# First attention of a two-layer attention and mixture-of-experts kernel: VectorE's share of a batch element's four steps dealt anew, the second normalisation moved to it, head outputs turned first

## The reference

```
x = x + xcond0(LN(x), ctx, tau, delta)       # softmax((q.k * tau + delta) / 4) over 375 keys, 16 heads
x = x + moe0(LN(x))                           # 64 experts, 8 chosen per token, sigmoid scores, plus a shared expert
x = x + xcond1(LN(x), ctx, tau, delta)
x = x + moe1(LN(x))                           # 8 experts, 2 chosen per token
```

## Time and profile before

| | |
|---|---|
| median of 3 runs | 1327.96 us (1319.44 to 1330.2) |
| the profiled execution | 1326.04 us, of which the span is 1324.4 us |
| TensorE busy | 1220.1 us, 92% |
| VectorE, GpSimd, ScalarE busy | 823.4, 557.1, 494.9 us |
| mean granted TensorE clock | 0.96 |
| GpSimd, mean of one normalisation (L1857), of one scatter (L1882) | 1254 ns, 968 ns |
| stages, from the span's start | attention 0 to about 377, experts to 676, attention to 1046, experts to 1324 |

### The profile page before, as it was taken

The page is one execution under the profiler, slowest core; times in us unless marked ns, Lnnn a source line. Parts: engine busy times, 40 slices in busy tenths (PEclk is TensorE's granted clock), DMA queues, the critical chain, the costliest instruction groups (busy, mean ns, idle before and its releaser), DMA issues. The chain is left out here.

```text
span 1324.4 us, 40274 instructions
## 1 busy us (share of the span) xinstructions
PE 1220.1 (92%) x12798; PEld 943.0 (71%) x12799; DVE 823.4 (62%) x2642; ACT 494.9 (37%) x1255; POOL 557.1 (42%) x706
## 2 busy tenths in 40 slices
PE   3899999999977999999888999999998999999995
PEld 2566666666644888898645666666666889999995
DVE  2357777877766666666564687777765544444442
ACT  1355454554430344443223544454544122122221
POOL 1116566665565000100356677776732313333231
PEclk8799999999978999999977999999998999999998
DMA  5343444446445668875423343333313313344323
GB/s 139 108 127 121 145 133 136 128 146 192 133 129 165 191 184 233 257 221 158 118 78 84 87 109 92 100 101 94 99 51 144 109 37 101 99 142 124 106 33 82
DMA packets 114268, 166.65 MB, mean 126 GB/s; under 512 B 26288, under 2 KB 95120, under 8 KB 113024
## 3 DMA queue, kind: packets, MB, share of 16 engines
q0 software_dynamic: 22672, 58.41, 17.0%
q1 hardware_dynamic: 46496, 54.35, 14.0%
q10 hardware_dynamic: 45024, 52.98, 12.6%
HBM read 87.82 MB, written 63.49 MB: 114 GB/s over the span
## 5 line engine op out<-in xcount | busy, mean ns | idle before, releaser
L1039 DVE TENSOR_REDUCE mx<-banks 112x2 f32<-112x750 f32 x256 | 235.3, 934 | 109.9 <-PE banks L625 96.8
L1882 POOL DMA_INDIRECT xs_d<-xns,idx x160 | 154.9, 968 | 136.6 <-PE banks L647 90.6
L1557 ACT ACTIVATE shared_buf<-banks 125x672 f32<-125x672 f32 x256 | 173.1, 728 | 104.3 <-PE banks L647 103.7
L1896 POOL DMA_INDIRECT kept<-y_d,yidx x128 | 124.7, 974 | 104.6 <-issue 83.3
L911 PEld LDWEIGHTS banks<-xT,attn_buf 128*128 128x128 f32 x1364 | 157.1, 192 | 4.8 <-DVE xT L1423 3.2
L911 PE MATMUL banks<-xT,attn_buf 128*128 128x128 f32 x1364 | 157.4, 275 | 3.0 <-DVE xT L1423 3.0
L856 PE MATMUL banks<-xT,staged 128*128 128x128 f32 x1064 | 142.7, 277 | 6.7 <-DVE staged L1434 6.2
L647 PE MATMUL banks<-attn_buf 18*125 18x112 f32 x3072 | 122.4, 290 | 24.7 <-DVE mx L1039 20.0
L856 PEld LDWEIGHTS banks<-xT,staged 128*128 128x128 f32 x1064 | 129.1, 192 | 11.6 <-DVE xT L1423 7.6
L647 PEld LDWEIGHTS banks<-attn_buf 18*125 18x125 f32 x3072 | 99.6, 189 | 53.0 <-DVE mx L1039 28.2
L625 PE MATMUL banks<-attn_buf 17*112 17x375 f32 x1024 | 119.7, 538 | 12.9 <-DMA attn_buf<-qT 10.1
(11 more groups left out here) (214 smaller groups left out, 1901.4 us busy)
## 6 DMA issues: line engine op xcount, KB each, us to landing
shared_buf<-xs_d SPq DMA_DIRECT2D x136, 128.0 KB, 2.4
y_d<-shared_buf ACTq DMA_DIRECT2D x132, 128.0 KB, 2.5
ringbuf<-in_we SPq DMA_DIRECT2D x6, 2176.0 KB, 8.2
ringbuf<-in_we POOLq DMA_DIRECT2D x32, 384.0 KB, 4.6
attn_buf<-attn_buf SPq DMA_DIRECT2D x128, 93.8 KB
attn_buf<-in_ctxT ACTq DMA_DIRECT2D x29, 375.0 KB
xs_d<-zrow ACTq DMA_DIRECT2D x16, 512.0 KB
y_d<-zrow ACTq DMA_DIRECT2D x16, 512.0 KB
```

Source lines behind the costliest of these rows:

```text
L1039: dve.tensor_reduce(mx[:, i % 2, 2 * p:2 * p + 2], banks[0:Q, 2 * p:2 * p + 2, 0:S], AX.X, ALU.max).then_inc(s_max, 1)
L1557: act.activation(pT[:, slot:slot + 2, :], banks[0:KT, first_bank:first_bank + 2, 0:ST * Q], ACT.Exp, scale=0.25).then_inc(s_exp, 1)
L1882: pool.indirect_dma_start(xs_d[L.number], bass.IndirectOffsetOnAxis(ap=idx[:, b % 2, k:k + 1], axis=0), rows, None).then_inc(s_scat[b % 2] ...
L1896: pool.indirect_dma_start(yg[:, u, k, :], None, y_d, bass.IndirectOffsetOnAxis(ap=yidx[:, u, k:k + 1], axis=0)).then_inc(s_gat[u][k * 4 // ...
```

## The change

Six edits, of which the second and third act in both attentions' code but matter in the first alone, and the first acts in both:

- `BEHIND`: `OT` is issued ahead of `Q`, and `OP` ahead of `V01`, in both layers.
- `WORK` of layer 0: `W81` goes ahead of `R0`; `R1` goes from step 1 (between the two halves of the maxima) to step 0, ahead of `OT`; `R2` goes ahead of the second half in step 1; `MOM2` goes from the end of step 1 behind the first half of the maxima in step 2; `LN2` is new in step 2, behind the second half.
- GpSimd's `normalise(1, ...)` in layer 0 becomes `deviation(1, ...)`: it makes `rstd` and no longer normalises.
- The multiplication of the 64 weights (`coef`, L1123) goes; the eight picked ones are multiplied instead, in the operation that copied them.
- Layer 0 picks six weights in `W80` and two in `W81`, instead of four and four. Layer 1 keeps one and one.

```diff
-        BEHIND = ((("Q", 2), ("OT", -1)), (("V01", 1), ("OP", -1)), (("K0", 2), ("XT2", -1)), (("K1", 2), ("LG", -1)))
+        BEHIND = ((("OT", -1), ("Q", 2)), (("OP", -1), ("V01", 1)), (("K0", 2), ("XT2", -1)), (("K1", 2), ("LG", -1)))
...
-                        for k in range(half, half + K // 2):
+                        for k in range(first, end):
                             into = xns1[:, u, k, D:D + 1] if l else w8row[:, k:k + 1]
-                            ins = dve.scalar_tensor_tensor(eq[:, k, 0:E], key[:, 0:E], p8[:, k:k + 1], coef[:, 0:E], ALU.is_equal, ALU.mult, accum_out=into)
+                            ins = dve.scalar_tensor_tensor(eq[:, k, 0:E], key[:, 0:E], p8[:, k:k + 1], (coef if l else wsel)[:, 0:E], ALU.is_equal, ALU.mult, accum_out=into)
...
-                        if l == 0 and half:
-                            link(after().tensor_copy(at(w8, b), w8row[:, 0:K]))
+                        if l == 0 and end == K:
+                            link(after().tensor_scalar(at(w8, b), w8row[:, 0:K], winv[:, 0:1], 2.5, ALU.mult, ALU.mult))
+
+                W8_PARTS = {"W80": (0, 1), "W81": (1, K)} if l else {"W80": (0, 6), "W81": (6, K)}
...
-                        link(after().tensor_scalar(coef[:, :], wsel[:, :], winv[:, 0:1], 2.5, ALU.mult, ALU.mult))
...
-                    WORK = ((("MAX", 0), ("R0", -2), ("W81", -3), ("OT", -1)),
-                            (("R1", -2), ("MAX", 0), ("R2", -2), ("R3", -2), ("OP", -1), ("MOM2", -1)),
-                            (("RK", -2), ("MAX", 0), ("MOM", 3)),
+                    WORK = ((("MAX", 0), ("W81", -3), ("R0", -2), ("R1", -2), ("OT", -1)),
+                            (("R2", -2), ("MAX", 0), ("R3", -2), ("OP", -1)),
+                            (("MOM2", -1), ("RK", -2), ("MAX", 0), ("LN2", -1), ("MOM", 3)),
                             (("SLOT", -2), ("MAX", 0), ("R4", -2), ("W80", -2)))
...
                     if in_layer(b, -1):
-                        normalise(1, n - 1, b - 1)
+                        deviation(1, n - 1)
```

More of the change, by code:

```diff
@@ L1054, in job @@
                     elif j == "LN2":
-                        dve.wait_ge(mm["XT2"], n - 1)
-                        dve.wait_ge(s_xns, n - 1)
+                        wait(dve, mm["XT2"], n - 1)
+                        wait(dve, s_xns, n - 1)
+                        hold(dve)
                         dve.wait_ge(s_rstd[1], n + 1)
@@ L1074, in job @@
                     elif j[:2] == "W8":
-                        half = int(j[2]) * K // 2
+                        first, end = W8_PARTS[j]
                         after()
-                        for k in range(half, half + K // 2):
+                        for k in range(first, end):
                             into = xns1[:, u, k, D:D + 1] if l else w8row[:, k:k + 1]
-                            ins = dve.scalar_tensor_tensor(eq[:, k, 0:E], key[:, 0:E], p8[:, k:k + 1], coef[:, 0:E], ALU.is_equal, ALU.mult, accum_out=into)
-                        if l and half:
+                            ins = dve.scalar_tensor_tensor(eq[:, k, 0:E], key[:, 0:E], p8[:, k:k + 1], (coef if l else wsel)[:, 0:E], ALU.is_equal, ALU.mult, accum_out=into)
+                        if l and end == K:
                             link_signal(ins, s_w8, b + 1)
```

## The result

The changed kernel takes 1334.18 us (median of 20 executions; lowest 1320.34) against 1324.57 us of the kernel before (20 executions, 1312.77 to 1330.2). The ratio is 1.0057, with a 95% interval of 1.0036 to 1.0078: +7.6 us (4.8 to 10.3). The ratio is worked out without one execution of 4832.77 us, at a mean granted clock of 0.24, and without two of 1343 us, more than 1.5% above the fastest. The profiled one took 1328.28 us, of which the span is 1326.4.

The account below looks back on a forecast made before the run. TensorE's queue was taken to set the length, other engines counting only where it waits. 8.7 - 1.4 + 2.3 - 4.8 = +4.8 us gave a forecast of 1332 us, range 1326 to 1338.

Parts of the forecast that it names:

- Step 0 into step 1, +0.67 us each: Layer 0: `R1` and other work ahead of step 1's maxima delay `scores_T` by 0.67 us in 13 bodies, +8.7 us.
- Step 1 into step 2, nothing: Layer 0: VectorE's later work there ends over a microsecond ahead of step 2's score rows, so nothing is paid.
- Step 2, a chain through `LN2`: Layer 0: maxima start sooner, but `XT2` waits for `LN2`; step 5.14 us long, -0.1 each over 14 bodies, -1.4 us.
- `LN2` beside the scatters: Layer 0, step 2: `LN2` takes 0.41 us; beside GpSimd's scatters up to 0.2 us more, 3 us in all.
- The rival of a collision: Layer 0: `LN2` waits for GpSimd's scatter, `XT2` 0.8 us later in 14 bodies, +11 us, 1343 us; chance 0.14.
- `Q`'s swap, +0.18 in layer 1: Layer 1, step 1: `Q`'s later eviction delays `max_T`, +0.18 us in 13 bodies, +2.3 us; hidden in layer 0.
- `OP`'s swap, -0.4: Layer 1, step 2: VectorE no longer waits for `OP`, `scores_T` comes sooner, -0.4 us in 12 bodies, -4.8 us.
- GpSimd, nothing: GpSimd loses 14 normalisations, costed at nothing, since nothing on the path waits for its other work.

Follow-up runs that it names:

- e2: Changed kernel with `R1` back between the halves of step 1's maxima and `R2` behind them: 1325.66 us, ratio 0.9927 to the kernel before.
- e6: Changed kernel with `R2` moved into step 0 as well, ahead of `OT`: 1372.16 us, ratio 1.0325 to the kernel before.
- e3: Changed kernel with `Q` ahead of `OT` again, `OP` staying ahead of `V01`: 1334.98 us, ratio 1.0062 to the kernel before.
- e9: Changed kernel with `MOM2` back at the end of step 1, `LN2` staying on VectorE: 1334.33 us, ratio 1.004 to the kernel before.
- e5: Changed kernel with GpSimd normalising again instead of `LN2`, all else kept: 1344.4 us, ratio 1.0131 to the kernel before.
- e7: Changed kernel with `V01` ahead of `OP` again, on the other chip: 1419.9 us, ratio 1.0016 to the kernel before.
- e8: e4's kernel with `OP` and `MOM2` ahead of `R3`, and `LN2` ahead of the second half: 1323.91 us, ratio 0.9983 to the kernel before.
- e1: Kernel before with TensorE's two swaps alone (`OT` ahead of `Q`, `OP` ahead of `V01`): 1321.46 us, ratio 0.9976.
- e4: Changed kernel with both `R1`'s move and `Q`'s swap undone: 1317.44 us, ratio 0.9918 to the kernel before.
- e12: Changed kernel with four unread matmuls ahead of `O2T` in step 1 of layer 0's last two bodies, other chip: 1411.98 us, ratio 1.000.

## Why the prediction was right

The forecast was 1332 us, within 1% of before, by +4.8 us; measured is a ratio of 1.0057, +7.6 us (4.8 to 10.3). That 1332 lies so near 1334.18 is in part luck: it was added to 1327.96, the median of three, and the median of twenty is 1324.57. The direction and the largest term are not luck. By the steps of the prediction:

- *Step 0 into step 1, +0.67 us each.* Measured +0.70 at the maxima and at `scores_T`, +0.69 in the step's length. e2 undid the move, and the maxima came 0.94 us earlier, to 1.08, the earliest of any step; e6 added to it, and they came 1.10 later. So there is no slack at this place, as the earlier trace rows showed in the wait of the weight load. The size has one correction: with the maxima on time `Q`'s eviction would still hold the step at 6.11, so of the 0.69 only 0.52 is what `R1` adds to it. That `Q`'s delay is hidden here was right (e3), and it works both ways.
- *Step 1 into step 2, nothing.* Right: step 2's maxima start at 1.08, with no wait for VectorE's earlier work.
- *Step 2, a chain through `LN2`.* 5.14 us were forecast, 5.07 came. The median step gained 0.23 rather than 0.1, because I scaled down from an early body of 4.97 us, while most bodies before the change were as the one in the earlier trace rows. e9 shows that the move of `MOM2`, which I took as the source of the gain, costs 0.31: what frees the maxima is that `OP` is earlier. e5 shows what `LN2` on VectorE saves once `MOM2` has moved (0.54 us). Whether it saves anything with `MOM2` where it was is not shown; no run has `OP` this early with both `MOM2` and the normalisation in their old places. By an estimate it doesn't: from the end of the moments to the end of GpSimd's `xn` it took 2.44 us in e5's body, which from the 1.00 of e9's body gives 3.44 us behind the score rows, and TensorE came to `XT2` there at 4.48. The prediction also had GpSimd's chain end with VectorE's; in the body of the earlier trace rows it ended at 185.31, and nothing waited for it. That credit was wrong, and the sum near enough.
- *`LN2` beside the scatters.* The times of its line in the changed kernel, shortest, median and longest in ns:

```profile
L1060 DVE TENSOR_SCALAR xn<-resid,mv,rstd x17: 401/404/412, 80.7 to 1043.3; 112x256 f32<-112x256 f32 x9, 112x256 f32 x8
```

  0.40 us always: in 12 of the 17 a scatter runs for the whole of it, as in the step 2 above (187.71 to 188.73), and these take 401 to 405 ns, the other five 402 to 412. The rival of a collision falls. The Trainium skill ("SBUF — State Buffer", "Who interferes with whom") has a VectorE instruction with one SBUF input and a GpSimd instruction exclude each other only if the first is in a two-port mode. At 404 ns, about the 420 of `OP`'s addition of the same size, which reads PSUM, no such mode shows, and the trace agrees with the rule to that extent.
- *`Q`'s swap, +0.18 in layer 1.* Step 1 lasts 0.21 more. But e3 shows that steps 0 and 2 give 0.14 and 0.15 back, and the body's cost is 0.09: I looked at one step only.
- *`OP`'s swap, -0.4.* Step 2 in layer 1 lasts 0.45 less, with the maxima 0.46 earlier; e7 takes it back (5.24 us, 1.73).
- *GpSimd, nothing.* Right.

Layer 0 from its body 2 to its end is 6.05 us longer, where 8.7 - 1.4 = 7.3 was forecast. Layer 1's twelve bodies are 1.7 us shorter by their means, where 2.5 was forecast. In sum +4.4 against +4.8. The profiled pair differs by 2.0 us only: the profile of before had two long steps in layer 1's bodies 1 and 14, both at a lowered clock (9.55 us at 0.56 where the changed kernel has 5.95, and 6.20 at 0.72 for 4.61). Such steps come and go between profiles: the first lasts 9.42 to 9.83 us in those of e2, e3, e5, e6, e8 and e9, and 6.13 to 6.26 in those of e1 and e4.

What the sum left out is the clock. Over all executions but the disturbed one, the time at half clock is 109.6 us in the median of the changed kernel and 101 to 103 in that of before, and an execution is longer by some 0.35 us for each of these: 2 to 3 us. By a line fitted to each kernel's executions, at an equal 105 us of half clock the two take 1331.5 and 1326.4 us, +5.1. Corrected in the same way (0.35 us for each, then the median), other differences come near those of the bodies too: e8 is 1.2 us above e4 instead of 6.5, and e9 is 3.0 us below the changed kernel instead of 0.1 above, where twelve bodies shorter by 0.24 give 2.9. This is a correlation over executions.

Which idle time lowers the clock is not shown. Body 14 of layer 0 was my candidate: in the profiles of e2, e3, e5 and e9 its step 1 lasts 8.75 to 10.30 us, much of it at half clock, in that of before 6.40 and in those of e4 and e8 6.11. But the changed kernel's own profile has it at 7.12 us and full clock, and e9's has the same idle times there and loses the clock:

```profile
346.60 0.39 PE L554 MATMUL banks<-con,o 112*128 112x112 f32 x2 [0.89 <-DVE o L1047]
347.45 1.61 PE L647 MATMUL banks<-attn_buf 18*125 18x112 f32 x24 [0.46 <-DVE mx L1039]
```

In e2 the clock had fallen near the start of the step (half clock from 341.62, the step from 340.77), behind idle times of 0.77 and 0.35 us in step 0 that e4 and the changed kernel have as well, at full clock. The same idle times lower the clock in one execution and not in another.

Two things stay open. On the other chip e4's gain over the kernel before is a loss; why VectorE starts step 0's maxima there 1.2 us late in most bodies wasn't found. The score rows were written at 0.90 in both cases, and VectorE's queue took up its wait for them at 0.97 on the first chip and at 2.13 to 2.23 in these bodies on the other, with no instruction between. And what decides whether a short idle time costs the clock.

## What to carry to other kernels

Where an engine's row of work ends directly at an operation that the bounding engine waits for, what is put ahead of it is paid in full, and two waits that end close together (here the maxima and `Q`'s eviction) must be removed together, or the second keeps part of the time. Before crediting a gain to a moved operation, look whether its input comes earlier for another reason; each part of a change is worth undoing by itself. A difference of under 1% in a kernel with short idle times on TensorE should be measured on a second chip, with the clock beside the time. And a run made to test a cause needs its own trace read: the clock in e12 had fallen before the place that was filled.

## What the runs showed of the hardware

TensorE's clock fell from 2.4 to 1.2 GHz behind short idle times in an otherwise full queue: in e6 behind 1.12 and 0.37 us, so that a delay of 1.1 us cost 2.8 us of step. The idle time alone doesn't decide it: 0.89 and 0.46 us in body 14 were followed by half clock in e9 and by full clock in the changed kernel. Another chip ran the same kernel before in 1411.35 us instead of 1326.6, at a mean clock of 0.93 instead of 0.96, and in the changed kernel VectorE started later at one place of most bodies there, while the medians of the other three steps of layer 0 were equal to a hundredth (6.63, 5.07, 5.41 us). A scatter of GpSimd and a fp32 operation of VectorE between SBUF tiles ran beside each other without a cost (401 to 405 ns in the 12 cases within a scatter).
